# Windowed attention feeding a mixture of experts: the query-key products of the next head are issued before the probability-value products of this one

## What is computed

```
xn  = layernorm(x)
# attention: 16 heads of 64, 8 windows of 256 queries; each sees its 256 keys
# and 128 on either side (at the two ends of the sequence only on one side)
q, k, v = split(xn @ w_qkv.T + b_qkv)
p   = softmax(q @ k.T / 8)            # per window and head
att = (p @ v) @ w_proj.T + b_proj
# mixture of experts: 8 experts, the two best of a gate weigh in
out_e = ((xn @ w0[e].T + b0[e]) * silu(xn @ w1[e].T + b1[e])) @ w2[e].T + b2[e]
out = x + att + sum over the top two of softmax(gate)[e] * out_e
```

## Time and profile before

| | |
|---|---|
| median of 9 runs | 3652.73 us (3627.72 to 4159.97) |
| the nine runs | 3627.72, 3629.12, 3630.29, 3633.1, 3652.73, 3740.6, 3808.64, 4080.33, 4159.97 us |
| the profiled execution | 3627.0 us, span of its slowest core (core 1) 3625.5 us |
| TensorE | busy 3190.9 us, 88% of the span |
| VectorE, ScalarE, GpSimd | 29%, 14%, 7% of the span |
| attention stage in the profile | first dots start at 374.57 us, the last VectorE instruction ends at 746.21 us |

### The profile page before, as it was taken

The page is one execution under the profiler, slowest core; times in us unless marked ns, Lnnn a source line. Parts: engine busy times, 40 slices in busy tenths (PEclk is TensorE's granted clock), DMA queues, the critical chain, the costliest instruction groups (busy, mean ns, idle before and its releaser), DMA issues.

```text
span 3625.5 us, 38153 instructions; the slowest of 8 cores (3611.8 to 3625.5 us)
## 1 busy us (share of the span) xinstructions
PE 3190.9 (88%) x15264; PEld 1484.2 (41%) x15264; DVE 1065.1 (29%) x1820; ACT 525.5 (14%) x665; POOL 256.5 (7%) x299
## 2 busy tenths in 40 slices
PE   2689555585999999999999999999999999999993
PEld 0634222241444444444444444444444444444441
DVE  3533322243223222422232233223222322332233
ACT  2100333300110121012101100110111012001200
POOL 0010000001110011011001100110010011001000
PEclk7589555586999999999999999999999999999996
DMA  3232000014631543063215314430543064143204
GB/s 113 82 36 35 1 1 1 1 24 52 69 37 12 70 39 38 1 82 38 27 25 69 37 16 64 41 36 6 76 41 30 9 80 41 18 61 38 24 24 162
DMA packets 310574, 150.16 MB, mean 41 GB/s; under 512 B 285296, under 2 KB 287728, under 8 KB 306296
## 3 DMA queue, kind: packets, MB, share of 16 engines
q0 software_dynamic: 304016, 113.84, 27.9%
q1 hardware_dynamic: 4656, 21.28, 1.7%
q10 hardware_dynamic: 1728, 12.58, 1.0%
HBM read 252.53 MB, written 8.45 MB: 72 GB/s over the span
## 4 chain that ended last, share of the span: by engine, by line
PE 86%; ACT 4%; DMA 4%; DVE 3%; issue 2%; DVEq 1%; ACTq 0%; SPq 0%; POOL 0%; POOLq 0%
PE pd L720 24%; PE pb L762 24%; PE pd L726 24%; ACT exp L574 4%; PE pd L567 3%; DMA xs<-xT 2%; PE pd L487 2%; PE pb L585 2%; PE pd L520 2%; PE pd L645 1%; PE pb L487 1%; DVEq L230 1%; DVE SUM L668 1%; PE pb L663 1%; DMA vsl<-wqkvT 0%
## 5 line engine op out<-in xcount | busy, mean ns | idle before, releaser
L720 PE MATMUL pd<-xn,w0sl 128*128 128x512 bf16 x4096 | 969.3, 379 | 21.1 <-DVE SUM L769 12.3
L726 PE MATMUL pd<-xn,w1sl 128*128 128x512 bf16 x4096 | 967.6, 379 | 0.0
L762 PE MATMUL pb<-act,W2T 128*128 128x512 bf16 x4096 | 885.3, 379 | 14.7 <-DVE act L741 14.7
L741 DVE SCALAR_TENSOR_TENSOR act<-pd,b0cols,sil 128x512 bf16<-128x512 f32 x512 | 384.5, 751 | 1409.2 <-ACT sil L735 1409.2
L735 ACT ACTIVATE sil<-pd,b1cols 128x512 bf16<-128x512 f32 x512 | 352.0, 688 | 2213.1 <-PE pd L726 2213.1
L720 PEld LDWEIGHTS pd<-xn,w0sl 128*128 128x128 bf16 x4096 | 400.5, 98 | 507.2 <-issue 26.5
L762 PEld LDWEIGHTS pb<-act,W2T 128*128 128x128 bf16 x4096 | 400.2, 98 | 499.8 <-issue 18.4
L726 PEld LDWEIGHTS pd<-xn,w1sl 128*128 128x128 bf16 x4096 | 400.8, 98 | 483.6 <-issue 0.6
L767 DVE TENSOR_TENSOR tmpb<-pb,gwb 128x512 f32<-128x512 f32 x256 | 177.1, 692 | 525.4 <-PE pb L762 525.4
L585 PE MATMUL pb<-V,exp 128*128 128x65 bf16 x960 | 72.9, 239 | 181.8 <-ACT exp L574 181.8
L190 POOL DMA_DIRECT2D w0sl<-w0T x128 | 112.1, 876 | 1633.8 <-PE pd L726 1509.3
(11 more groups left out here) (81 smaller groups left out, 695.5 us busy)
## 6 DMA issues: line engine op xcount, KB each, us to landing
w0sl<-w0T POOLq DMA_DIRECT2D x128, 256.0 KB, 4.4
w1sl<-w1T POOLq DMA_DIRECT2D x128, 256.0 KB, 5.2
W2T<-w2T POOLq DMA_DIRECT2D x8, 4096.0 KB, 29.5
xs<-xT SPq DMA_DIRECT2D x12, 1024.0 KB, 7.2
xs<-xT ACTq DMA_DIRECT2D x12, 1024.0 KB, 6.2
outT<-ob SPq DMA_DIRECT2D x8, 1024.0 KB, 4.8
qksl<-wqkvT POOLq DMA_DIRECT2D x16, 256.0 KB, 4.4
gwb<-gw_scratch POOLq DMA_DIRECT2D x8, 512.0 KB, 30.4
```

What stands on the lines that cost most here:

```text
L720: step("tensor", lambda t, s=slot, dt=dt, tc=tc, par=par: t.matmul(pb[par * 2][:], w0sl[s][:, dt * 128:(dt + 1) * 128], xn[dt][:, tc * 512 ...
L726: h_mm_done[(e, ht)] = step("tensor", lambda t, s=slot, dt=dt, tc=tc, par=par: t.matmul(pb[par * 2 + 1][:], w1sl[s][:, dt * 128:(dt + 1) * ...
L741: act_evac[(e, i)] = step("vector", lambda v, ht=ht, tc=tc, par=par, bcol=bcol: v.scalar_tensor_tensor(out=act[ht][:, tc * 512:(tc + 1) * ...
L762: b_last_mm = step("tensor", lambda t, ht=ht, dt=dt, tc=tc, bk=bk: t.matmul(pb[bk][:], W2T_sb[:, ht * D + dt * 128:ht * D + dt * 128 + 128 ...
```

## The change

The loop body is split into three functions over a list of the 128 iterations, with the same instructions, buffers and waits in each: `emit_dots` (TensorE's dots), `emit_exp` (ScalarE's exponential) and `emit_av` (TensorE's AV and VectorE's work). The loop then calls them in another order: the dots of iteration it+1 are written ahead of the AV of iteration it.

```diff
+    def emit_dots(it):
+        ...
+        if it >= 3:
+            rec.wait("tensor", cs, dots_free[par])
+        ...
+        dots_done_l[it] = dd
+
+    def emit_exp(it):
+        ...
+        rec.wait("scalar", ct, dots_done_l[it])
+        if it >= 3:
+            rec.wait("scalar", ct, exp_free[par])
+        exp_done_l[it] = step("scalar", lambda s, e=par, par=par, nk=nk: s.activation(
+            out=expb[e][:, 0:nk * 256], in_=pd[par][:, 0:nk * 256],
+            func=AF.Exp, bias=c_shift[:], scale=1.0 / 8.0), cs)
+        dots_free[par] = exp_done_l[it]
+
+    def emit_av(it):
+        ...
+        rec.wait("tensor", cs, exp_done_l[it])
+        if it >= 2:
+            rec.wait("tensor", cv, av_free[it % 2])
+        ...
+        rec.wait("vector", ct, av_done)
+        ...
+        av_free[it % 2] = ev
+
+    emit_dots(0)
+    for it in range(NIT):
+        emit_exp(it)
+        if it + 1 < NIT:
+            emit_dots(it + 1)
+        emit_av(it)
```

More of the change, by code:

```diff
@@ L547, in build_program @@
     barrier()
+    iters = []
+    for g in range(NG):
+        klist = [kt for kt in range(2 * g - 1, 2 * g + 3) if 0 <= kt < NTT]
+        for h in range(NH):
+            iters.append((g, h, klist))
+    NIT = len(iters)
     dots_free = {}
@@ L551, in build_program @@
     exp_free = {}
[L552 to L564, removed]
-            for j, kt in enumerate(klist):
[L566 to L603, removed]
@@ new lines, in build_program @@
+    dots_done_l = {}
+    exp_done_l = {}
+    def emit_dots(it):
+        g, h, klist = iters[it]
+        par = it % 3
+        pt = h // 2
+        po = (h % 2) * 64
+        nk = len(klist)
+        if it >= 3:
+            rec.wait("tensor", cs, dots_free[par])
+        dd = 0
+        for j, kt in enumerate(klist):
+            dst = pd[par][:, j * 256:(j + 1) * 256]
+            dd = step("tensor", lambda t, d=dst, pt=pt, po=po, kt=kt, g=g: t.matmul(
+                d, kT[pt][po:po + 64, kt * 128:(kt + 1) * 128],
+                qT[pt][po:po + 64, g * 256:(g + 1) * 256],
+                start=True, stop=True), ct if j == nk - 1 else None) or dd
+        dots_done_l[it] = dd
@@ new lines, in emit_exp @@
+    def emit_exp(it):
+        g, h, klist = iters[it]
+        par = it % 3
+        nk = len(klist)
+        rec.wait("scalar", ct, dots_done_l[it])
[6 more added lines that the diff above has]
+    def emit_av(it):
+        g, h, klist = iters[it]
+        par = it % 3
+        abk = 6 + it % 2
+        nk = len(klist)
+        rec.wait("tensor", cs, exp_done_l[it])
+        if it >= 2:
+            rec.wait("tensor", cv, av_free[it % 2])
+        av_done = 0
+        for qi in range(2):
+            for j, kt in enumerate(klist):
+                last = (qi == 1 and j == nk - 1)
+                av_done = step("tensor", lambda t, e=par, j=j, qi=qi, kt=kt, abk=abk, h=h, nk=nk: t.matmul(
+                    pb[abk][:, qi * 65:qi * 65 + 65],
+                    expb[e][:, j * 256 + qi * 128:j * 256 + qi * 128 + 128],
+                    Vaug[kt][:, h * 65:(h + 1) * 65],
+                    start=(j == 0), stop=(j == nk - 1)), ct if last else None) or av_done
+        exp_free[par] = av_done
+        rec.wait("vector", ct, av_done)
+        ev = 0
+        for qi in range(2):
+            rcc = (it % 2) * 2 + qi
+            step("vector", lambda v, abk=abk, qi=qi, rcc=rcc: v.reciprocal(
+                rc_sb[:, rcc:rcc + 1], pb[abk][:, qi * 65 + 64:qi * 65 + 65]))
+            ev = step("vector", lambda v, abk=abk, qi=qi, g=g, h=h, rcc=rcc: v.tensor_scalar(
+                out=AO[g * 2 + qi][:, h * 64:(h + 1) * 64],
+                in0=pb[abk][:, qi * 65:qi * 65 + 64],
+                scalar1=rc_sb[:, rcc:rcc + 1], scalar2=None, op0=ALU.mult),
+                cv if qi == 1 else None, dr=True) or ev
+        av_free[it % 2] = ev
```

## The result

The changed kernel takes 3447.35 us (median of 10 runs, lowest 3443.7), against a median of 3631.98 us for the kernel before over the 31 runs then at hand. The ratio is 0.949, with a 95% interval of 0.9478 to 0.9502. The profiled execution took 3447.2 us against 3627.0: 180 us less. (Some executions of either kernel run longer, with a lower mean clock on the cores of one die or of both; the ratio compares the others, which is why 3447 stands against some 3630 and not against the first nine runs' 3653.)

What follows compares the result with a forecast made beforehand. Attention was taken as bound by a circle of waits between TensorE and ScalarE. At full clock its 371.6 us become 147.8, gain 223.8; 3627.0 becomes 3403, plus 13 for the median 3416 us; range 3394 to 3472.

Steps and rivals of the forecast that it cites:

- The circle of waits: Attention stage: exponential, AV, dots, exponential wait on each other, 3.03 us a turn, 2.49 with three blocks; stage 371.6 us.
- The circle halves: Attention stage: two chains side by side, 1.515 us per iteration at half clock; stage 187.7 us, gain 183.9.
- Rival B: Attention stage: TensorE's clock stays at half; gain 183.9 us, total 3456 with the median's 13; chance 0.25.
- TensorE's need of 2 x 1.38 per turn: Attention at half clock: two AV groups of 0.53 and two dots groups of 0.85 us, 2.76 within 3.03.
- The clock: TensorE in attention: columns streamed rise from 510 to 1019 per us, so full clock is likelier than half.
- A: Attention stage: TensorE rises to full clock; gain 223.8 us, total 3416, own range 3394 to 3441; chance 0.47.
- The stage at full clock: Attention: circle 2.33 us over two iterations, 1.165 per iteration, 1.05 with three blocks; stage 147.8 us, gain 223.8.
- Company on PSUM: ScalarE's exponential in attention: reading PSUM while TensorE and VectorE use other banks costs nothing measurable; it stays at 1.114 us.
- The 13 us added for the median: Whole kernel: half of the 25.7 us between the nine runs' median, 3652.73, and the profiled execution, added to 3403.
- C: Attention stage: clock goes back and forth, half the time at each; gain 203.8 us, total 3436; chance 0.24.
- D: Attention stage: the waits don't loosen, the turn stays at 3.03 us; total 3640; chance 0.02.
- E: Attention and experts: the chip's current limit lowers the granted clock; slower, 4065 us at clock 0.81; chance 0.02.

Runs made afterwards that it cites:

- experiment 1: The changed kernel with dots issued two iterations ahead of their AV instead of one; 3443.67 us, ratio 0.9479 to the kernel before.
- Experiment 2: The changed kernel with each dots matmul reading 128 rows instead of 64, so summing two heads' products; 3402.3 us in one run.
- experiment 7: The changed kernel with 128-row dots (two heads summed) in windows 0, 2, 4, 6 and 64-row dots in the others; 3420.35 us in one run.
- experiment 4: The changed kernel with every 64-row dots matmul issued twice; total 3545 to 4086 us, first to last exponential 283.7 us on core 0, 179.3 on core 3.
- experiment 9: The changed kernel with all attention matmuls on rows 0 to 63, AV leaving out each block's upper 64 keys; 3440.6 us in one run.
- experiment 3: The changed kernel with 128-row dots (two heads summed), issued two iterations ahead; 3385.84 us in the profiled execution.
- experiment 5: The changed kernel with full results from 128-row dots, GpSimd copying q into zero-padded buffers, dots two iterations ahead; 3385.11 us, ratio 0.9315 to the kernel before.
- experiment 8: The kernel before, in its own order, with 128-row dots (two heads summed); 3620.3 us in one run.
- experiment 10: The changed kernel with all attention matmuls on rows 0 to 63 and dots two iterations ahead; 3412.3 us in one run.

## Why the prediction was right or wrong

*What bounds the kernel: right.* The circle of waits, its 3.03 and 2.49 us, and its place on every core's path. The gain came from this stage, and all but some 3 us of it reached the end. (The fastest core of that profile was core 6 with 3611.8 us and not core 2 with 3612.1; nothing hangs on it.)

*The circle halves: right, and within a microsecond, with some luck.* At half clock the prediction had 187.7 us for the stage and a gain of 183.9; measured are 188.4 and 183.2. Rival B's sum from the profile, 3443, stands against 3447.2 in the profiled execution and a lowest run of 3443.7. The luck is that TensorE's own need, which the sum had wrong, came out no longer than half a turn: a little more of it, and the circle would not have set the time.

*TensorE's need of 2 x 1.38 per turn, with 0.27 to spare: wrong.* The 0.53 for AV, read from starts, held one switch of rows (its columns alone are 0.43); the 0.85 for the dots, 1.03 less the 0.18 of a last matmul's latency, left out the other. TensorE's need is 2 x 1.52 (experiment 1), with nothing to spare. It cost the forecast nothing, as the two limits are equal, but it misleads on a deeper look-ahead: by it experiment 1 was promised a stage of about 172 us, some 16 below the changed kernel's 188, and brought about 4.

*The clock: wrong, and this is the step that failed.* "I take the full clock as the likelier" carried A and with it the 3416. The granted clock was 0.50 from some 4 us into the stage to its end, and the time is that of rival B, to which 0.25 was given; that 3447 lies in the range is B's doing and not A's. The argument counted columns per us (1019 after, against 510) and set the half-filled rows aside as a point "against it". Experiment 2 changes the rows alone and gets 1.00 with 45 us less; experiment 7 turns the clock on and off with them; experiments 4 and 9 exclude the switches. Had I weighed it as the deciding one, the forecast would have been B. The profile of before didn't hold the answer: no stretch of it has matmuls of 64 rows packed as densely as the change packs them.

*The stage at full clock: the circle was right, the needs of ScalarE and VectorE too long.* It can be read in experiment 2, where the clock is full: 141.2 us from first to last exponential, where the prediction's sum has 145.4 without its two ends. The circle is right, 2.30 for two iterations against 2.33. ScalarE's need of 1.114 and a pause is wrong: back to back it is 1.01. VectorE's 0.97 and a pause, 1.05, is 0.87 in experiment 3. So the low end of 3394, worked out from ScalarE alone at 1.114, was no floor: the kernel of experiment 5 takes 3385.

*Company on PSUM: right.* The exponential takes 1113 ns on the mean with AV, dots and VectorE beside it, against 1114.

*The 13 us added for the median: too much.* They came from the spread of nine runs. Over 31 runs the median is 5 us above the profiled execution, over ten of the changed kernel it is 0.1. B with 5 us instead of 13 would have read 3448.

*The rivals.* C, back and forth, did not occur in the changed kernel: the clock fell once, on every core. That both states can hold for the same instructions, experiment 4 shows. D and E fell: the turn opened, and the experts kept clock 1.00 in 2678.5 us with TensorE in attention busy 97%, and also behind an attention stage at full clock in experiment 5. The Trainium skill's rule that three dense cores of a die bring the clock down to 13/16 (TensorE: Matmul & The Clock Gate, Part 1) would have these rows of the experts at 0.81; their 1.00 disagrees again.

*Pauses.* The kernel of experiment 8 has the rows of experiment 2 and, in the old order, 1.47 us of idle in each turn; it stays at 0.50. The Trainium skill's rule that pauses between bursts of matmuls cost the clock (TensorE: Matmul & The Clock Gate, HAM oscillation) agrees with that, though its example has longer waits. Pauses don't explain the changed kernel, which has next to none and 0.50 too: there the measurement shows a second condition, the rows.

## What to carry to other kernels

When a stage is a circle of waits across engines, work out the turn from starts in the timeline and divide by the iterations that the new order puts into it; then work out each engine's own need at the clock it will have, with the switches between kinds of matmul included, and take the larger. A look-ahead in the order of instructions cost nothing here, since the buffers for it were already there, and it halved the stage. TensorE's clock is a separate question that neither its busy share nor its columns answers: matmuls that use 64 of 128 rows kept it at 1.2 GHz in this stage with next to no pauses, and padding the rows with zeros, if an idle engine can do it, is worth trying on the chip (here, with one more iteration of look-ahead, it was worth 62 us).

## What the hardware showed that was not expected

- With 64-row dots TensorE stood at half clock while busy 97 to 100% of the stage; with 128-row dots, half of the streamed ones zeros, it rose to full clock and stayed there while busy about 80% (experiment 5). In experiment 4, with twice the 64-row dots, five cores stood at half clock all through and one at full clock, on the same instructions. That the rows decide in the changed kernel is shown; where the border lies is open.
- Going from matmuls of 128 rows to such of 64, or back, costs some 0.11 us each time at half clock (1.52 us per iteration with two switches, 1.30 without, experiments 1 and 10). At full clock AV to dots is 0.27 us for six AV with the switch and 0.18 without it in experiment 3, so 0.09.
- ScalarE's exponential of 1024 columns takes 1.114 us alone and 1.01 back to back (experiment 3).
